# Edges listed by halves of 64 rows, and gathered tiles shared between two buckets, in a fused graph layer

## The reference, cut to what matters

```python
xn = _layernorm(x, axis=-1)                                    # x: 6250 x 256, f32
x = x + _L0_gnn_ref(xn, edge_weight, src, dst) + _L0_mix_ref(xn[None], Wqkv, ...)[0]
...
def _L0_gnn_ref(x, values, row, col):                          # 100,000 edges
    msgs = values[:, None] * x[col]
    out = jax.ops.segment_sum(msgs, row, num_segments=N_NODES)
```

## Time and profile before

| | |
|---|---|
| median of the runs shown | 2158.93 us |
| the profiled execution, its own time | 2159.11 us |
| its span in the profile | 2157.3 us |
| TensorE busy | 1852.7 us (86%) |
| VectorE busy | 1407.6 us (65%) |
| GpSimd busy | 1317.4 us (61%) |
| ScalarE busy | 1128.4 us (52%) |
| mean granted TensorE clock | 0.91 |

### The profile page before, as it was taken

The page is one execution under the profiler, slowest core; times in us unless marked ns, Lnnn a source line. Parts: engine busy times, 40 slices in busy tenths (PEclk is TensorE's granted clock), DMA queues, the critical chain, the costliest instruction groups (busy, mean ns, idle before and its releaser), DMA issues.

```text
span 2157.3 us, 41674 instructions
## 1 busy us (share of the span) xinstructions
PE 1852.7 (86%) x11902; PEld 1251.0 (58%) x11950; DVE 1407.6 (65%) x3497; ACT 1128.4 (52%) x3220; POOL 1317.4 (61%) x1258
## 2 busy tenths in 40 slices
PE   5676767899999999799999999987756999999940
PEld 3454553555555555445455444445756898999940
DVE  8999998887777777455555566765663444433347
ACT  4765653454444445365665666654632444455434
POOL 2233435777777777777777777772773666544434
PEclk8688987899999999999999999997558999999975
DMA  5333101333333333333333343385764555555565
GB/s 189 109 130 129 30 27 36 99 99 100 101 101 100 100 100 101 105 113 111 113 113 111 113 123 111 113 101 134 241 226 94 99 101 101 102 104 106 103 198 217
DMA packets 150077, 248.13 MB, mean 115 GB/s; under 512 B 25312, under 2 KB 109410, under 8 KB 149922
## 3 DMA queue, kind: packets, MB, share of 16 engines
q0 software_dynamic: 64496, 144.32, 27.8%
q1 hardware_dynamic: 82466, 99.36, 14.6%
q10 hardware_dynamic: 2960, 2.57, 0.4%
HBM read 182.25 MB, written 63.91 MB: 114 GB/s over the span
## 4 chain that ended last, share of the span: by engine, by line
PE 54%; POOL 15%; DVE 12%; issue 8%; DMA 7%; ACT 3%; SPq 0%; DVEq 0%; POOLq 0%; ACTq 0%
POOL big L855 12%; PE b L1955 10%; PE bqk L2237 8%; PE bank L2217 8%; DMA big<-xn_dram,big 5%; PE bank L2093 4%; PE bqk L2104 3%; POOL z_dram L864 3%; PE bqk L2009 2%; PE b L1971 2%; PE bank L1900 2%; PE b L2207 1%; PE bank L1985 1%; PE bqk L1882 1%; DVE st L1235 1%
## 5 line engine op out<-in xcount | busy, mean ns | idle before, releaser
L855 POOL DMA_INDIRECT big<-xn_dram,big x832 | 828.9, 996 | 255.4 <-issue 230.1
L1955 PE MATMUL b<-big 128*128 128x256 f32 x1468 | 395.6, 394 | 29.8 <-DMA big<-xn_dram,big 27.0
L1955 PEld LDWEIGHTS b<-big 128*128 128x128 f32 x1468 | 259.2, 191 | 197.8 <-issue 102.8
L884 POOL DMA_INDIRECT sum_dram<-mid,idxy x113 | 176.4, 1561 | 227.4 <-DMA sum_dram<-mid,idxy 124.9
L998 ACT ACTIVATE big<-big 128x128 f32<-128x128 f32 x832 | 265.7, 403 | 37.2 <-DVE big L1465 18.9
L2217 PEld LDWEIGHTS bank<-late,mid 128*128 128x128 f32 x1808 | 219.4, 193 | 9.8 <-issue 5.0
L2217 PE MATMUL bank<-late,mid 128*128 128x128 f32 x1808 | 223.2, 277 | 0.0
L2237 PE MATMUL bqk<-big,mid 128*128 x896 | 215.7, 384 | 0.0
L1490 DVE TENSOR_TENSOR acc<-acc,b 128x256 f32 x251 | 104.9, 418 | 154.3 <-PE b L1955 118.5
L1069 ACT ACTIVATE big<-bank 128x512 f32<-128x512 f32 (+1 forms) x208 | 102.3, 577 | 165.5 <-PE bank L2093 165.5
L2237 PEld LDWEIGHTS bqk<-big,mid 128*128 128x128 f32 x896 | 161.2, 190 | 20.7 <-issue 0.2
(11 more groups left out here) (348 smaller groups left out, 3356.6 us busy)
## 6 DMA issues: line engine op xcount, KB each, us to landing
big<-w SPq DMA_DIRECT2D x32, 512.0 KB
mid<-z_dram SPq DMA_DIRECT2D x114, 130.0 KB, 2.1
mid<-b SPq DMA_DIRECT2D x113, 128.0 KB, 3.4
big<-xn_dram,big POOLq DMA_INDIRECT x832
sum_dram<-mid SPq DMA_DIRECT2D x19, 640.0 KB, 4.0
big<-sum_dram SPq DMA_DIRECT2D x18, 640.0 KB, 13.1
acc<-x_pad SPq DMA_DIRECT2D x10, 640.0 KB, 6.6
xn_dram<-big SPq DMA_DIRECT2D x9, 640.0 KB, 3.4
```

What stands on the lines that cost most here:

```text
L855: pool.indirect_dma_start(out=gx[t % GB], out_offset=None, in_=xn_dram, in_offset=bass.IndirectOffsetOnAxis(ap=dstA[:, t:t + 1], axis=0)). ...
L884: pool.indirect_dma_start(out=sum_dram[t % 2], in_=yo[t % 4], in_offset=None, out_offset=bass.IndirectOffsetOnAxis(ap=idxy[t % 4][:, 0:1], ...
L1955: a = pe.matmul(to[:, 0:C], wd[t % (2 * EB)], gx[t % GB], start=(e == unit[0] and j == 0), stop=(e == unit[-1] and j == 1), skip_group_che ...
```

## The change

The records are now listed in half rows of 64 edges (`HP` = 64). A bucket's count of halves is split into groups of 16, 8, 4, 2 and 1, so a tile of 128 is two consecutive halves of one bucket, and the odd half of a bucket is listed at the end. Two odd halves share one gathered tile: edges of one bucket on partitions 0 to 63, of another on 64 to 127. The bounds become `OCTS` 208, `QUADS` 306, `PAIRED` 354, `SOLO` 378 and `EP` 404: pairs 0 to 207 in fours, 208 to 305 in twos, 306 to 353 alone, 354 to 377 with two adds, and 378 to 403, 26 **shared pairs**, with four buckets and four adds. That is 808 tiles and 52 + 49 + 48 + 48 + 104 = 301 adds. A shared pair is four matmuls (eight MATMUL records) of 64 rows: both tiles' lower halves into bank 0, then both upper halves into bank 1, each bank after a wait of its own.

In `sort_finish` there are five classes, 245 table entries and 15 comparisons, where the last two of the 13 record fetches are two indirect DMAs each, of half rows. The core of the diff:

```diff
-EP = 416
+EP = 404
-OCTS, QUADS, PAIRED = (-(-(TILES - k * NBK) // (k + 1)) * (k + 1) // 2 for k in (7, 3, 1))
+OCTS, QUADS, PAIRED, SOLO = (-(-(HALVES - k * NBK) // (k + 1)) * (k + 1) // 4 for k in (15, 7, 3, 1))
+HG = 2 * SOLO // 64
+FRG = NRB + NRB - HG
-PERS = (9, 9)
-ENT = 4 * NBK
+PERS = (9, 8)
+ENT = 5 * NBK
...
+def listed():
+    order = list(range(QP))
+    units = [[e for e in range(u, u + 4) if e >= QP] for u in range(QP - QP % 4, OCTS, 4)]
+    units += [[e, e + 1] for e in range(OCTS, PAIRED, 2)]
+    rest = [[e, e + 1] for e in range(PAIRED, EP, 2)]
+    for i, unit in enumerate(units):
+        order += unit
+        for more in rest[i * len(rest) // len(units):(i + 1) * len(rest) // len(units)]:
+            order += more
+    return order
...
+        if what == "edge" and LISTED[i] >= SOLO:
+            side[what, i], need[what, i], last = 0, held[:], 1
+            held = [ADDS[p] + 2, ADDS[p + 1]]
+            continue
...
+            for g in range(HG, NRB):
+                for k in range(2):
+                    at = g + k * (NRB - HG)
+                    pool.indirect_dma_start(out=rg[g][:, HP * k:HP * (k + 1)].bitcast(I32), out_offset=None, in_=rec_halves,
...
             def edge(e):
-                if e == unit[0] and OPEN["edge", e]:
+                whole = LISTED[e] < SOLO
+                if whole and e == unit[0] and OPEN["edge", e]:
                     pe.wait_ge(s_add, OPEN["edge", e])
                 for j in range(2):
...
+                    if not whole:
+                        if j == 0 and OPEN["edge", e][0]:
+                            pe.wait_ge(s_add, OPEN["edge", e][0])
+                        a = pe.matmul(ps_pair[0][:, C * j:C * (j + 1)], wd[t % (2 * EB)][0:HP, :], gx[t % GB][0:HP, :],
+                                      start=True, stop=True, skip_group_check=True)
...
+                if not whole:
+                    for j in range(2):
+                        t = 2 * e + j
+                        if j == 0 and OPEN["edge", e][1]:
+                            pe.wait_ge(s_add, OPEN["edge", e][1])
+                        a = pe.matmul(ps_pair[1][:, C * j:C * (j + 1)], wd[t % (2 * EB)][HP:P, :], gx[t % GB][HP:P, :],
+                                      start=True, stop=True, skip_group_check=True)
                 a.then_inc(s_pair, 1)
```

More of the change, by code:

```diff
@@ L138, with unit_edges @@
 PAIRS = len(ORDER)
-def unit_edges(e):
+def listed():
[7 more added lines that the diff above has]
+            order += more
+    assert sorted(order) == list(range(EP))
+    return order
+LISTED = listed()
+def unit_edges(i):
+    e = LISTED[i]
     n = 4 if e < OCTS else 2 if e < QUADS else 1
-    first = e - (e - (0 if e < OCTS else OCTS)) % n
+    first = i - (e - (0 if e < OCTS else OCTS)) % n
     return range(first, first + n)
@@ L844, in _ @@
             rec_rows = rec_dram.rearrange("(l r) o -> l (r o)", r=P)
-            for g in range(NRB):
+            rec_halves = rec_dram.rearrange("(l r) o -> l (r o)", r=HP)
+            for g in range(HG):
                 pool.indirect_dma_start(out=rg[g].bitcast(I32), out_offset=None, in_=rec_rows,
@@ L1421, in sort_finish @@
                 v.tensor_tensor(idxt[:], off, tailw, ALU.add).then_inc(s_idxt, 1)
[L1422 to L1425, removed]
+                classes = [slice(NBK * i, NBK * (i + 1)) for i in range(5)]
+                link(v.tensor_scalar(fcupI, fsel, 63.0, None, ALU.add))
+                link(v.tensor_scalar(fcupI, fcupI, 6, None, ALU.arith_shift_right))
+                for i, bits in enumerate((2032, 8, 4, 2, 1)):
                     mark(v.tensor_scalar(fncolI[:, classes[i]], fcupI, bits, None, ALU.bitwise_and))
@@ L1429, in sort_finish @@
                 link(v.tensor_tensor(fbeg, fend, fncolI, ALU.subtract))
[L1430 to L1438, removed]
+                link(v.tensor_tensor(frow.rearrange("p (i b) -> p i b", i=5), bval.unsqueeze(1).broadcast_to([P, 5, NBK]),
+                                     fbeg.rearrange("p (i b) -> p i b", i=5), ALU.subtract))
+                for j in range(4):
+                    for i in range(j + 1, 5):
+                        mark(v.tensor_tensor(frow[:, classes[i]], frow[:, classes[i]], fncolI[:, classes[j]], ALU.add))
+                    join()
                 mark(v.tensor_tensor(fbeg[:, 0:ENT - 1], frow[:, 0:ENT - 1], frow[:, 1:ENT], ALU.subtract))
@@ L1442, in sort_finish @@
                 join()
-                for g in range(NRB):
+                for g in range(FRG):
                     mark(v.scalar_tensor_tensor(out=ohs[g % 2].rearrange("p t s -> p (t s)")[:, ENT * (g // 2):ENT * (g // 2 + 1)],
@@ L1489, in collect_edge @@
                         v.wait_ge(s_add, ADDS[p] + j)
-                    v.tensor_tensor(mine, mine, ps_pair[SIDE["edge", e]][:, C * j:C * (j + 1)], ALU.add).then_inc(s_add, 1)
+                    v.tensor_tensor(mine, mine, ps_pair[side][:, C * half:C * (half + 1)], ALU.add).then_inc(s_add, 1)
             def add_bias(b):
@@ L1936, in turn_records @@
                 for g in range(NRB):
-                    pe.wait_ge(s_rg[g // 2], 16 * min(2, NRB - g // 2 * 2))
+                    pe.wait_ge(s_rg[g // 2], 16 * sum(1 if i < HG else 2 for i in range(g // 2 * 2, min(g // 2 * 2 + 2, NRB))))
                     if g >= 2:
```

89 lines of the change are left out of this document (53 added, 36 removed).

## The result

The changed kernel took 2191.7 us (median of 4 runs, 2189.9 to 2192.9), the kernel before 2159.3 us on the same chip (4 runs, 2154.5 to 2159.9): a ratio of 1.0159, 95% interval 1.0145 to 1.0173, or 32.4 us slower. The forecast was 2175.5, 16.4 us slower: the right side, just inside the range of 2151 to 2192, but half the size. Run again on another occasion it took 2194.4 against 2157.9 us (ratio 1.0166, interval 1.0146 to 1.0186). The profiled execution spans 2189.9 us, 32.6 more than the one of before.

What follows compares the result with a forecast made beforehand. Gathers hold the key stage; in the query stage TensorE is packed without holes and GpSimd nearly full. -10.2 - 8 - 2 + 2.6 + 2.6 + 28.8 + 2.6 = +16.4 on 2159.1 gives 2175.5 us, range 2151 to 2192.

Steps and rivals of the forecast that it cites:

- Taken away: Query stage: twelve pairs fewer -10.2 us, fewer gathers and their waits -8, waits of pairs with two adds -2.
- waits in z = 2, 6 and 10: Gap 0 of these halves: a unit directly behind the add of its bank, 3 x 0.85 = +2.6 us.
- third rival: Query stage: the gathers still bind, so the -8 falls away; near 2178 us, chance 0.05.
- Before the key stage: Two more record fetches and a longer VectorE chain, +2.6 us (2.5 to 3.5); first gather at about 380.5.
- The shared pair itself: Query stage: row groups run side by side, about 1.07 us for 0.98, 26 x 0.1 = +2.6 us.
- second rival: Shared pairs: halves don't run side by side, +12 us (2187.5) or +17.6 (2193); chance 0.22.
- The waits for banks: Query stage: shared pairs hold both banks long, so TensorE waits for adds; +28.8 us, bounds nothing to about 40.
- the classes: Waits sorted by what stands before or behind a shared pair, each bank-free time less covering work; sum +28.8 us.
- 2 to 5 was named as the sign: Halves 13 to 19 should each be 2 to 5 us longer than their like.
- first rival: Query stage: waits for banks mostly covered, 2144 us, or 2154.5 with a third of them; chance 0.24.
- the fourth: Rival: it comes out even, waits about half as large as counted, 2159 to 2162 us; chance 0.07.
- The sum: All terms added, +16.4 us on 2159.1, giving 2175.5 us, 0.8% slower; chance 0.42.

Runs made afterwards that it cites:

- Experiment 1: The changed kernel with its 26 shared pairs multiplied as full-height pairs in one bank with two adds, leaving out the parting of shared tiles: 2138.3 us, ratio 0.989.
- experiment 9: The changed kernel with two of each shared pair's four adds left out, matmuls unchanged: 2159.3 us, ratio 0.9997.
- experiment 3: The changed kernel reordered, one shared pair in gap 4 of each of the 26 halves, before 3.3 us of other work: 2140.0 us, ratio 0.990.
- experiment 6: The kernel with one shared pair in gap 4 of each half, plus a TensorE wait behind each for its four adds: 2278.4 us, against 2140.0 without.

## Why the forecast had the side right and half the size

**Taken away.** -10.2, -8 and -2 us make 20.2. Experiment 1, which still has the waits in z = 2, 6 and 10, is 22.6 us faster in the medians (2161.0 to 2138.3); in the profiles its halves 1 to 24 are 17.4 us shorter than before (551.8 to 534.4), 20.8 with the 3.4 us of those waits taken out. The odd halves are 20.27 us (forecast: 20.3), half 23 has no wait for a gather and is 7.45 us shorter. Right, and the third rival, gathers that still bind, is out.

**Before the key stage.** +2.6 was not there, nor was the first gather at 380.5: in fourteen profiles with the new sort it starts at 378.8 in the mean, in two of before at 378.4. The two more fetches are issued, but the profiles of one kernel differ by as much as they cost.

**The shared pair itself.** Side by side, as the nearer row (`select`) said, and with its 1.07 us from start to start; but the block behind takes 0.11 more too, which no term had. That makes 0.21 for each pair, about 5 us, not 2.6. The second rival, with the halves one after the other, is out. The Trainium skill says that matmuls start strictly in order (TensorE: Matmul & The Clock Gate, Part 3, "The mechanism"). The trace does not agree for these: in the program all lower matmuls stand ahead of the upper ones, and the first upper record starts 0.02 us after the first lower one, 0.3 us before the second lower one.

**The waits for banks.** They came where the classes put them. Less the clock, the halves 13 to 23 are 34.4 us longer than their like without shared pairs (20.27 and 24.74 us); up to 5 of it are the pairs' own 0.2 us each, and the sum of the waits was 28.8. Against the same halves of experiment 1 it is 32.3. Half by half: 3.1, 3.6, 3.8, 4.9, 3.6, 6.1, 2.0, 2.6, 0.7, 3.0, 1.0 us from z = 13 to 23, and the classes give about 2.3, 3.7, 3.0, 4.1, 4.1, 4.6, 3.7, 0.5, 0.5, 1.8, 1.0. Right in sum, less so one by one. With the clock, the halves 13 to 19 are 3.1 to 8.8 us longer, where 2 to 5 was named as the sign. The waits in z = 2, 6 and 10 cost 3.4 us, forecast 2.6. The first rival, in which they are covered, is out, and so is the fourth.

**The step that failed is "The sum".** It priced each wait by its length alone and had no term for TensorE's clock; the only clock of the stage that I had read was 1.00, and one matmul of 1.69 us behind a 2.36 us wait was the hint, booked as part of the gathers. Taken half by half, from 1 to 24 the kernel is 28.8 us longer (551.8 to 580.6), of which the clock is 12.2 (13.9 less 1.7); the last half and its end are 4.4 us longer, some 2 of them clock: the lower level begins at 1507.8, and from `answer_rest` to TensorE's next work behind the stage it is 10.4 us, 8.3 before. That is some 14 us of the 16 that were missing. The rest of the stage grew by 16.6 where the forecast has 13.8 (16.4 less the 2.6 ahead of the key stage) for the whole of it.

That 2191.7 still lies inside the range is luck. The range reached to 2192 for the sake of the second rival, halves that don't run side by side, and the runs show that they do; nothing in it stood for the clock.

That the waits bring the clock down is shown: one wait of about 3 us in each half does it 25 times in 26, experiment 9 with short waits has a quarter of the loss, and experiments 1 and 3 without waits have none. That they account for all of it is not: with the same waits and full-height records the clock costs 7.2 and 10.7 us where the changed kernel has 13.9 and 15.3. What is over goes with the 64-row matmuls, though they do nothing alone in the halves 1 to 24 (experiment 3); what it is stays open.

## What to carry to other kernels

A wait of TensorE for a bank has two prices: its length and, where it is as long as the 3 us of experiment 6 or where several shorter ones stand close together, about half again in clock. Read the granted clock by windows of a few us around each wait that a change adds, and don't take it from a stage that has none. Where a unit of work holds both banks for long, one of them in each stretch, ahead of other work that is as long as its adds, turned 32 us of loss into 21 us of gain with the same matmuls and adds.

## What the runs showed that was not expected

- A wait of 1.4 to 1.8 us, alone in its half, left the clock at 1.00 in 18 of 18 cases; one of 2.5 us in 4 of 5; one of 3.3 us in none of 5; one of 2.9 us and more in each half in 1 of 26. The short last two halves are left out of this: there the lower level comes in the end even without such a wait (experiment 3, from 1460.5 us).
- Two sets of fp32 matmuls in the two halves of the rows start in turn, 0.02 us apart, even if the program has four records of the one ahead of four of the other; eight such records cost 0.10 us more than four of full height, and the full-height block behind them 0.11 more.
- In the changed kernel's last half, where matmuls are 128 columns wide and two shared pairs stand close, the clock up to the end of the work was 0.76 and 0.78 in two profiles, and 1.00 in three with full-height records and waits in the same places.
